# A decoder stack of 16 tiles on one core: transposed inner values in the first feed-forward stage, and its first steps moved ahead of the last attention steps

## The reference, cut to what matters

```python
def _ternary_linear(x, w):                     # w is replaced by its ternary form
    d = x.shape[-1]
    rms = sqrt(sum(x * x, -1)) / sqrt(d)
    return einsum('bsd,fd->bsf', x / (rms + 1e-8), w_q)
h = gelu(_ternary_linear(layernorm(x), w_up), approximate=False)    # 128 -> 512
x = x + _ternary_linear(h, w_down)                                  # 512 -> 128
```

## Time and the profile before

| | us |
|---|---|
| median of 3 runs | 485.76 |
| the runs | 483.43 to 486.47 |
| the profiled execution, whole | 484.05 |
| its span, first to last instruction | 482.1 |

### The profile page before, as it was taken

The page is one execution under the profiler, slowest core; times in us unless marked ns, Lnnn a source line. Parts: engine busy times, 40 slices in busy tenths (PEclk is TensorE's granted clock), DMA queues, the critical chain, the costliest instruction groups (busy, mean ns, idle before and its releaser), DMA issues.

```text
span 482.1 us, 15833 instructions
## 1 busy us (share of the span) xinstructions
PE 443.4 (92%) x5607; PEld 330.5 (69%) x5607; DVE 407.8 (85%) x1316; ACT 374.4 (78%) x1467; POOL 252.5 (52%) x354
## 2 busy tenths in 40 slices
PE   3988999999978999999999999999999999999971
PEld 2645565666655777877888877787787787787750
DVE  4698888888857897699879989989989989889984
ACT  1686879889964556599898898898888888888951
POOL 2366897787666662023523534544544453545584
PEclk9998899999999999999999999999999999999997
DMA  8032000000000001878656754844854754758000
GB/s 239 11 103 99 7 13 12 5 10 7 8 2 1 0 1 42 207 195 193 140 119 131 178 120 103 194 116 97 191 119 103 175 127 113 161 139 186 16 7 22
DMA packets 54366, 44.73 MB, mean 93 GB/s; under 512 B 43936, under 2 KB 49312, under 8 KB 54304
## 3 DMA queue, kind: packets, MB, share of 16 engines
q1 hardware_dynamic: 53728, 43.26, 37.6%
q10 hardware_dynamic: 576, 0.65, 0.4%
HBM read 22.92 MB, written 20.97 MB: 91 GB/s over the span
## 4 chain that ended last, share of the span: by engine, by line
PE 66%; DVE 16%; POOL 6%; issue 5%; ACT 4%; DMA 2%; SPq 1%; DVEq 0%; POOLq 0%; ACTq 0%
PE PS L961 56%; PE PS L969 5%; PE PS L1126 4%; POOL rstd L332 3%; ACT prob L410 1%; DMA relr<-rel_scratch 1%; ACT fin L567 1%; DVE xf L815 1%; DMA ctx<-in_ctxT 1%; POOL prob L297 1%; DVE prob L792 1%; DVE uo L878 1%; DVE xn L765 1%; DVE ve L769 0%; PE PS L1228 0%
## 5 line engine op out<-in xcount | busy, mean ns | idle before, releaser
L343 POOL TENSOR_TENSOR prob<-prob,rsum 128x480 f32<-128x480 f32 x64 | 65.2, 1019 | 120.1 <-DVE rsum L809 43.3
L483 ACT ACTIVATE prob<-prob,nmax 128x120 f32<-128x120 f32 x256 | 98.2, 391 | 0.9 <-DVE nmax L890 0.6
L410 ACT ACTIVATE prob<-PS,nmax 128x120 f32<-128x120 f32 x256 | 88.8, 409 | 3.3 <-DVE nmax L639 3.2
L297 POOL TENSOR_TENSOR prob<-prob,rsum 128x480 f32<-128x480 f32 x64 | 62.4, 989 | 28.3 <-DVE rsum L688 14.3
L410 ACT ACTIVATION_READ_ACCUMULATOR prob<-PS,nmax 128x1 f32 x256 | 65.6, 256 | 0.0
L961 PE MATMUL PS<-rT,qv 64*32 64x152 f32 x2048 | 45.9, 294 | 6.0 <-ACT fin L567 5.9
L483 ACT ACTIVATION_READ_ACCUMULATOR prob<-prob,nmax 128x1 f32 x256 | 50.5, 197 | 0.0
L969 PEld LDWEIGHTS PS<-ident,prob 128*120 128x120 f32 x256 | 28.1, 139 | 30.3 <-POOL prob L297 12.2
L961 PEld LDWEIGHTS PS<-xnT,wq 128*128 128x128 f32 x288 | 37.7, 194 | 13.3 <-issue 10.2
L961 PE MATMUL PS<-xnT,wq 128*128 128x128 f32 x288 | 43.8, 290 | 1.2 <-DMA ctx<-in_ctxT 1.1
L969 PE MATMUL PS<-ident,prob 128*120 128x128 f32 x256 | 37.8, 282 | 7.1 <-DVE v L648 3.1
(11 more groups left out here) (192 smaller groups left out, 1105.7 us busy)
## 6 DMA issues: line engine op xcount, KB each, us to landing
rel_scratch<-relw SPq DMA_DIRECT2D x128, 152.0 KB, 2.6
relr<-rel_scratch SPq DMA_DIRECT2D x64, 240.0 KB, 4.3
ctx<-in_ctxT SPq DMA_DIRECT2D x32, 60.0 KB, 1.9
out_x<-fin SPq DMA_DIRECT2D x16, 64.0 KB, 1.6
x_all<-in_x SPq DMA_DIRECT2D x1, 704.0 KB, 7.6
wr<-in_wr SPq DMA_DIRECT2D x1, 512.0 KB, 5.8
wq<-in_wq SPq DMA_DIRECT2D x1, 512.0 KB, 3.6
wk<-in_wk SPq DMA_DIRECT2D x1, 512.0 KB, 4.4
```

The costliest lines, as they stand in the source:

```text
L297: return pool.tensor_tensor(pr, pr, cols(rsum[p], g, HG).unsqueeze(2).to_broadcast([S, HG, SK]), ALU.mult)
L343: return pool.tensor_tensor(pr, pr, cols(rsum[p], g, HG).unsqueeze(2).to_broadcast([S, HG, SK]), ALU.mult)
L410: last = act.activation(cols(prob[p], n, SK), cols(scores, q, SK), ACT.Exp, bias=nmax[p][:, n:n + 1], accum_out=ssum[p][:, n:n + 1])
L483: last = act.activation(cols(pr, n, SK), cols(pr, n, SK), ACT.Exp, bias=bias[:, n:n + 1], accum_out=total[:, n:n + 1])
```

## The change

The up-product is formed transposed: four chunks of `wup` are stationary, one after the other, and `xnT` moves, so that bank 2 or 3 holds the inner values with the feature on the partition. ACT's Gelu writes `hidT` straight from it. The transposes of `hid` and the copy to `hidT` go. For the sum of squares ACT now squares `hidT` into `hid`, DVE adds the four chunks (`tensor_reduce` over a view whose innermost step is 128 elements, 512 bytes) into 128 partial values per partition, PE sums these over the partitions with a one-column product against `per_ff`, ACT copies the column to `ve2`, and POOL takes the root. This takes one step more, so tile t is finished in step t+3, and ffn0 has a step 18. On POOL the second root now stands ahead of the first in a step.

The border is reordered, and steps 4 and 5 of ffn0 are peeled too.

```diff
-LOOPS = ((6, 12), (4, NB - 4), (8, NB - 4))
+LOOPS = ((6, 12), (6, NB - 4), (8, NB - 4))
...
-            for s in range(3):
-                peeled(ffn0, s - 3, s - 2)
-                peeled(attn0, NB + 1 + s, NB + 2 + s)
-            peeled(ffn0, 0, LOOPS[1][0])
+            peeled(ffn0, -3, -2)
+            peeled(ffn0, -2, -1)
+            peeled(ffn0, -1, 0)
+            peeled(ffn0, 0, 1)
+            peeled(attn0, NB + 1, NB + 2)
+            peeled(ffn0, 1, 2)
+            peeled(attn0, NB + 2, NB + 3)
+            peeled(ffn0, 2, LOOPS[1][0])
...
+            peeled(ffn0, NB + 2, NB + 3)
             peeled(layer1, 0, LOOPS[2][0])
...
+                if on(s - 3):
+                    t, p = s - 3, 1 - par
+                    act.wait_ge(F0["ssq_ps"], t + 1)
+                    after(act, F0["rms"], t - 1)
+                    act.activation(ve2[p][:, :], PS[:, 4 + p, 0:1], ACT.Copy).then_inc(F0["ssq"], 1)
...
+                    act.activation(hidT[par][:, :], PS[:, 2 + par, :], ACT.Gelu).then_inc(F0["gelu"], 1)
+                if on(s):
+                    act.wait_ge(F0["gelu"], s + 1)
+                    after(act, F0["sums"], s - 1)
+                    act.activation(hid[par][:, :], hidT[par][:, :], ACT.Square).then_inc(F0["squares"], 1)
...
+                t1, p1 = s - 1, 1 - par
+                if on(t1):
+                    dve.wait_ge(F0["squares"], t1 + 1)
+                    after(dve, F0["ssq_ps"], t1 - 1)
+                    dve.tensor_reduce(out=cols(hsq, p1, S), in_=hid[p1][:, :].rearrange("p (c s) -> p s c", c=4),
+                                      op=ALU.add, axis=AX.X).then_inc(F0["sums"], 1)
...
-                    dve.tensor_tensor_reduce(out=hsq[:, :], in0=hid[par][:, :], in1=hid[par][:, :],
-                                             scale=1.0 / DFF, scalar=0.0, op0=ALU.mult, op1=ALU.add,
-                                             accum_out=ve2[par][:, :]).then_inc(F0["ssq"], 1)
...
-                    mm(PS[:, 2 + par, :], xnT[par][:, :], wup_sb[:, :]).then_inc(F0["up_ps"], 1)
+                    for c in range(4):
+                        last = mm(PS[:, 2 + par, c * S:(c + 1) * S], cols(wup_sb, c, D), xnT[par][:, :])
+                    last.then_inc(F0["up_ps"], 1)
...
-                    for c in range(4):
-                        last = pe.transpose(PS[:, 4 + p, c * S:(c + 1) * S], cols(hid[p], c, D), ident_sb[:, :])
-                    last.then_inc(F0["hidT_ps"], 1)
...
+                    pe.wait_ge(F0["sums"], t + 1)
+                    after(pe, F0["ssq"], t - 1)
+                    mm(PS[:, 4 + p, 0:1], cols(hsq, p, S), per_ff[:, :]).then_inc(F0["ssq_ps"], 1)
```

More of the change, by code:

```diff
@@ L171, in decoder_kernel @@
         F0 = {n: sem("f0_" + n) for n in (
-            "stats", "var", "root", "den", "xn", "xnT_ps", "xnT", "up_ps", "gelu", "ssq", "rms", "hidT_ps", "hidT",
+            "stats", "var", "root", "den", "xn", "xnT_ps", "xnT", "up_ps", "gelu", "squares", "sums", "ssq_ps", "ssq", "rms",
             "down_ps", "den2", "x_done")}
@@ L327, in ffn0 @@
             def ffn0(s, par):
+                t, p = s - 3, 1 - par
+                if on(t):
+                    pool.wait_ge(F0["ssq"], t + 1)
+                    after(pool, F0["den2"], 2 * t - 3)
+                    pool.tensor_tensor(rstd2[p][:, :], ve2[p][:, :], half[:, 0:1], ALU.pow).then_inc(F0["rms"], 1)
                 if on(s + 3):
@@ L467, in ffn0 @@
                     act.activation(xnT[p][:, :], PS[:, p, 0:S], ACT.Copy).then_inc(F0["xnT"], 1)
[L468 to L472, removed]
+                if on(s):
+                    act.wait_ge(F0["up_ps"], s + 1)
+                    after(act, F0["down_ps"], s - 1)
+                    act.activation(hidT[par][:, :], PS[:, 2 + par, :], ACT.Gelu).then_inc(F0["gelu"], 1)
+                if on(s):
+                    act.wait_ge(F0["gelu"], s + 1)
+                    after(act, F0["sums"], s - 1)
+                    act.activation(hid[par][:, :], hidT[par][:, :], ACT.Square).then_inc(F0["squares"], 1)
             def layer1(s, par):
@@ L750, in ffn0 @@
                     dve.wait_ge(A0["xnT_ps"], NB)
-                if isinstance(s, int) and s < 1:
-                    dve.wait_ge(A0["x_done"], t3 + 1 if s < 0 else NB)
+                if isinstance(s, int) and s < 6:
+                    dve.wait_ge(A0["x_done"], t3 + 1 if s < 5 else NB)
                 if on(t3):
@@ L1098, in ffn0 @@
                     pe.transpose(PS[:, p, 0:S], xn[p][:, :], ident_sb[:, :]).then_inc(F0["xnT_ps"], 1)
-                if on(s - 1):
-                    t, p = s - 1, 1 - par
+                if on(s - 2):
+                    t, p = s - 2, par
+                    if at_step(t, 0):
+                        pe.wait_ge(setup_g, 4)
+                        pe.wait_ge(A0["oT"], 16)
+                        pe.wait_ge(A0["x_done"], 16)
+                    pe.wait_ge(F0["gelu"], t + 1)
+                    after(pe, F0["x_done"], t - 1)
+                    for c in range(4):
+                        last = mm(PS[:, 6 + p, 0:D], cols(hidT[p], c, S), cols(wdn_sb, c, D),
+                                  start=(c == 0), stop=(c == 3))
+                    last.then_inc(F0["down_ps"], 1)
                     if at_step(t, 0):
```

38 lines of the change are left out of this document (10 added, 28 removed).

## The result

The changed kernel takes 491.49 us (median of 18 runs, 488.17 to 494.74 without one disturbed run of 676.43), the kernel before 482.38 (18 runs, 481.38 to 486.47): ratio 1.0172, 95% interval 1.0141 to 1.0203. The profiled execution took 493.1 with a span of 491.1; before it was 484.05 and 482.1. The forecast was 484.7 and no change; the time fell where rival 1 had put it, though, as will be seen, only in part for rival 1's reason.

A forecast was written before the change was run, and what follows sets the result against it. DVE-POOL-DVE ring (2.26 us) and PE (2.30) bound the peeled step, afterwards DVE (2.18). Steps, loop and tail summed to `rel` starting 1.06 us sooner: 484.05 - 1.06 = 482.99 profiled, 484.7 median; range 482.5 to 493.5.

The forecast's parts named there:

- rival 1: DVE's strided reduction costs two cycles a value, 1.14 us each, giving 492.9 by the median; chance 0.33 full, 0.07 partial.
- The strided reduction: DVE's sum of 512 values with a step of 512 bytes, taken at 0.61 us from start to start.
- Steps 12 to 14 ... unchanged: End of ffn0: these steps lose the ring's waits, gain exposed latency, and keep their 5.34 us.
- the tail of 7.00: DVE's work after those steps to its last addition: 6.15 - 0.40 + 0.61 + 0.64 us.
- The ring DVE, POOL, DVE at 1.81: Chain through POOL's root in each ffn0 step, shortened from 2.26 to 1.81 us, with the root at 0.70 instead of 1.13.
- PE's step 2.12: PE's work per ffn0 step: 1.00 up-product and transpose, 0.89 down-product, 0.23 one-column product; before 2.30 us.
- Rival 2: PE stays the bound because the one-column product costs 0.4 us, PE's step 2.29; time 486.3, chance 0.10.
- DVE's front part 0.93: DVE's work in an ffn0 step ahead of the reduction, 0.93 us as before.
- the peeled step 2.18: DVE's own work becomes the bound of a written-out ffn0 step, 2.18 us against 2.26 before.
- the looped 2.45: A step in ffn0's hardware loop takes 2.45 us, between bounds 2.29 and 2.52; before 2.39.
- The border: Between attn0 and ffn0 the reordering puts step 1 at 149.55 instead of 149.92, a gain of 0.37 us.
- ACT and POOL cost nothing: ACT can carry the square and one-column copy, and POOL's second root ahead of the first is costed at nothing.

The follow-up runs named there:

- Experiment 1: Changed kernel with DVE's reduction summing four neighbouring values, so other values than the reference: 485.44 us, ratio 1.0056 to the kernel before.
- Experiment 9: Changed kernel with the last two down-products of ffn0 in the up-products' PSUM banks: 487.97 us, ratio 1.0099 to the kernel before.
- 6: Changed kernel with nine spare PE products ahead of the last two down-products of ffn0: 489.47 us, ratio 1.0157 to the kernel before.
- 2: Changed kernel with ACT writing the squares interleaved, so DVE sums neighbours with the reference's values: 486.43 us, ratio 1.0093 to the kernel before.
- experiment 3: Changed kernel with the attn0 and ffn0 border steps in the old order: 493.30 us, ratio 1.0234 to the kernel before.
- 12: Changed kernel with end-of-stage repairs, steps 6 to 9 written out, three ways for the squares: 483.88, 483.54, 484.20 us; the third with the old border 481.70.

## Why the prediction was wrong

- **The strided reduction: mis-sized, and the larger cause.** "I take 0.61, because it is the only rate that the rows show for 512 values" gave 0.61; it is 0.96, two thirds of the way to the 1.14 of rival 1. Experiment 1 shows it alone. The rule that spoke for rival 1, of the Trainium skill (Advanced Engine Details and Errata, SBUF Cachelines), is borne out: a step that leaves the line of 16 bytes costs DVE (0.68 to 1.04), ACT (0.63 to 1.12) and the weight load (192 to 327 ns). No run tried a step that stays within such a line, so where the price begins is not shown. I gave rival 1 0.33 where the one instruction without a row near it was also the only one that the change put on the bound engine 16 times.
- **"Steps 12 to 14 ... unchanged" and the tail of 7.00: the step that failed.** The tail was summed on DVE alone. With the reduction fast, these two still take 6.62 and 10.7 in place of 5.34 and 7.04. The forecast missed that a down-product waits for DVE's `x_all` of two tiles before, that the added pipeline step moves that read a step later, and that layer1's products stand behind the last one-column product. Experiment 9 shows the wait by taking it away. That the fall of the clock at the end belongs to it is not shown: the clock is full in the profiles of 6 and 9, but also in that of 2, where PE waited 0.85 and 1.06, while it is half in that of 1 behind waits of 0.83 and 0.97.
- **The ring DVE, POOL, DVE at 1.81, root 0.70: right** (root(t) of steps -3 to 0: 139.14, 140.96, 142.77, 144.59).
- **PE's step 2.12: right.** Its parts: 0.97 and 0.11 for up-product and transpose, 0.90 for the down-product, 0.14 for the one-column product, which had been given 0.23. Rival 2 did not come.
- **DVE's front part 0.93, the peeled step 2.18, the looped 2.45: right for a fast reduction** (2.16 and 2.44 in experiment 1).
- **The border: the place was right (10.48 and 10.49), the reading wrong.** With these shorter steps the old order puts step 1 in the same place (experiments 3 and 12), so the 0.37 came from the ring (step 0 takes 1.83 without `hsq` in experiment 3, 2.19 with it in the kernel before), not from the order. That the new order leaves PE idle for 2.87 and lowers its clock was not in the forecast.
- **ACT and POOL cost nothing: right** but for 0.4 us that DVE waits for ACT's squares in all, as long as ACT reads and writes without a step.
- **Rival 1's 492.9 against 491.49:** nearly the number, but 16 reductions at 0.35 are 5.6 us at the most and not 8.2, and the rest came from the end of the stage. The agreement of the total is chance.

What stays open is how much of the 0.7% of experiment 9 is the wait and how much the clock, and what makes the clock fall at the end in one execution and not in another. Five of the changed kernel's runs had a mean clock of 0.970 or 0.971, the profiled one among them, and took 493.1 to 494.7; the other twelve, at 0.977 to 0.982, took 488.2 to 491.7. So the 2.6 us of half clock read from the profile are not to be carried over to the median. The ring over two tiles was read from a trace and cut in one place only; it was not cut by a third buffer for Gelu's output.

## What to carry to other kernels

When a change gives an instruction an access pattern that no row shows, and puts it on the bound engine once per step, its price is the forecast; price it at the slow end or measure it alone. When a stage gets one pipeline step more, follow every buffer that is freed a step later, above all at the end of the stage, where no other work covers the wait. And compare profiles from the nearest point that both share: a lower clock on the border moved everything behind it by 0.6 us, as much as some of the repairs. And what is cheap for one engine (PSUM written with a step by PE) can be dear for the next that touches the same data (its weight load).

## What the hardware showed that was not expected

- 512 fp32 values with a step of 512 bytes: DVE 1.04 against 0.68 us, ACT 1.11 against 0.63; with a step of 16 bytes where ACT writes, 1.13. On ACT it did not matter which of the two steps it was.
- PE writes PSUM with a step of 16 bytes at no cost. The Trainium skill (PSUM — Partial Sum Buffer, Specifications (TRN2)) says that any non-contiguous pattern slows matmuls significantly; for these writes the runs say otherwise, and the measurement decides.
- One-column fp32 products take 0.10 us a pass in a row of eight, as much as passes of 128 columns.
- Beside two DVE additions with two SBUF operands each (256 and 128 columns) POOL's root takes 0.08 us longer, beside `hsq` with 512 columns 0.43.
- With the new order of the border, which leaves PE idle for 2.87 us, the granted clock over 139 to 150 was 0.69 to 0.84 in every profile, with the old order 1.00.
